# Sums of products by accumulating transfers, differences in place, and a projection with seven columns a head

## The chip, the cores and the metric

The kernel runs on one core of a Trainium2 chip. What is measured is the device time of one execution in microseconds. Differences of about 0.5% of this kernel's time can't be told from no change.

## The reference

Sixteen images x of 64 channels and 64x64 pixels, all in fp32. First three residual steps with two 3x3 convolutions, then a linear-attention block with eight heads of eight channels:

```python
for _ in range(3):
    t = jax.nn.relu(_conv(x, w1) + b1[None, :, None, None])
    x = x + (1.0 / 3.0) * (_conv(t, w2) + b2[None, :, None, None])
x = jax.nn.relu(x)

def _ln(t, w, b):                      # over the 8 channels of a head
    m = t.mean(-1, keepdims=True)
    s = jnp.std(t, axis=-1, ddof=1, keepdims=True)
    return w * ((t - m) / (s + EPS)) + b
qkv = jnp.einsum('oc,bchw->bhwo', qkv_w, x)        # -> q, k, v per head
k, v = _ln(k, kln_w, kln_b), _ln(v, vln_w, vln_b)
kv = jnp.einsum('bhnd,bhne->bhde', k, v) / N
o = jnp.einsum('bhnd,bhde->bhne', q, kv)           # heads back to channels
ret = o + x
u = gelu(jnp.einsum('oc,bchw->bohw', o1_w, ret))
return gelu(jnp.einsum('oc,bchw->bohw', o2_w, u) + x)
```

## The kernel before

**Tiles.** Two images make a pair: 128 partitions are two images of 64 channels. There are eight pairs, three x tiles in a ring (`xs`), one tile t between the two convolutions of a step, and one program of ten iterations. In each iteration a pair enters (step 0), the pair before it is in steps 0 and 1, and the one before that in step 2 and in its attention; so convolutions of one pair stand beside the attention of another.

**Phases and gaps.** An iteration has six phases with 42 gaps in all (`GAPS`); in each gap TensorE runs one unit of a convolution or half a unit. CONV0 (x to t) is a direct convolution of nine taps (line 956) in "long" units, or in its "short" half by products. CONV1 (t to x's increment dx) is by products throughout. A product half takes a column of input rows, spreads it on VectorE into six planes v (SPREAD, lines 711 to 771), multiplies the planes on TensorE (line 982 for CONV1, 989 for the short half of CONV0) in three parts of two planes, and merges the six results into four output rows on VectorE (MERGE, lines 786 to 829). ScalarE drains each part out of PSUM: parts 0 and 1 into `m`, part 2 into `m_ends` (lines 551 to 554). `m` is a single buffer: the next half's part 0 waits until the sums have been made from it. MERGE starts with two operations of 128x1024, sum and difference of the halves of m (lines 793, 794), into `sums`.

**Attention steps.** PIXELS (line 586, ScalarE) copies x, PROJECT k (line 1021, TensorE) makes k and v of an eighth of the pixels with the pixels as stationary operand and the 128 columns of `kvw` as moving one, ScalarE copies them to `kv` (598) and squares them (606), VectorE sums the squares of each head (836). The mean is taken out by the weights beforehand, so that only the deviation is left to be made: DEVIATION (610), INVERT (843 to 850), NORMALISE (855). OUTER (1033, TensorE) makes k'v, the four FOLD steps (1042 to 1050, with copies on VectorE at 859 to 871) turn it into a matrix, UP and DOWN (1064, 1073) apply it and the second weight with a gelu (618) between, VectorE adds x (881), FINISH (623) is the last gelu, RELU (591) the relu of x. In PSUM the convolutions have two buffers of two banks; the attention uses one slot in turn, and three in the last iteration.

**Order.** Each engine runs one hand-made order. The tables CONV_PLACES (for SPREAD, MERGE and RECTIFY of each half, by pair 0, pairs 1 to 6, pair 7) and LATE, LAST, FINAL (for the attention of pairs 0 to 5, of pair 6, of pair 7) give each step a gap as a number; within a gap the numbers order them. Every engine takes the steps in that order, and semaphores do the rest.

**GpSimd's queue.** GpSimd issues the additions of dx to x: two accumulating transfers a half (line 494), one for each side, in the order in which dx is made. The convolution of the next step waits for them (`x_added`). x comes in by SP's queue in four chunks of two transfers; w1 by two transfers on ScalarE's queue. The first unit of a pair waits for chunks 0 and 1.

## Time and profile before

| | us |
|---|---|
| median of the runs (1300.70, 1303.31, 1306.62) | 1303.31 |
| the profiled run | 1304.89 |
| its span | 1303.1 |
| TensorE busy in it | 1188.0 |
| VectorE busy | 1085.5 |
| ScalarE busy | 597.4 |
| GpSimd busy | 91.1 |
| granted clock, mean (1.00 is 2.4 GHz) | 0.967 |

The span is the time from the first to the last instruction in the trace; 1.8 us of the profiled run lie outside it. Busy times say how long an engine had an instruction under way. Matmuls overlap in TensorE, so a mean duration of one record is longer than what it adds to the time; what counts is the distance from one line's first start to the next line's. The stretches of 150 us from 350 to 1100 are alike, each a little more than one pair; the first 350 us hold the start and the last 200 the drain of the pipeline.

### The profile page before, as it was taken

What the parts mean: (1) busy time and instruction counts of PE and PEld (TensorE: products, weight loads), DVE (VectorE), ACT (ScalarE), POOL (GpSimd) and SP (SyncE); (2) the same over time, 40 slices, a digit from 0 to 9 for tenths busy, and PEclk for the clock granted to TensorE, in tenths of its full rate; (3) what the DMA queues carried; (4) which work ended last, traced back from release to release, by engine and by line L of the source; (5) the groups of instructions that cost most, each with busy time, mean ns of one, the idle gap of its engine ahead of it and who ended that gap; (6) DMA issues with size and microseconds to landing.
All of it is one profiled execution on the core that took longest, in us unless ns stands there. A gap on an engine that the chain in (4) does not pass through costs nothing. (4 is left out here: it accounts for less than half of the span.)

```text
span 1303.1 us, 40508 instructions
## 1 busy us (share of the span) xinstructions
PE 1188.0 (91%) x18613; PEld 805.4 (62%) x18613; DVE 1085.5 (83%) x1425; ACT 597.4 (46%) x642; POOL 91.1 (7%) x119
## 2 busy tenths in 40 slices
PE   6989999999999999999999999999999999785845
PEld 2546766577556766676566875676665875445432
DVE  3658888899888998899988997989978998987563
ACT  0212324454455626544455625554455625544573
POOL 2010110001010100101000100101000110110000
PEclk9989999999999999999999999999999999897876
DMA  7430330315061513515061422515061330430221
GB/s 131 91 68 1 69 68 2 68 36 102 18 150 33 102 36 99 101 36 102 2 164 35 86 52 70 129 35 102 2 163 36 69 69 34 100 68 2 82 51 65
DMA packets 87130, 88.95 MB, mean 68 GB/s; under 512 B 70320, under 2 KB 70320, under 8 KB 86960
## 3 DMA queue, kind: packets, MB, share of 16 engines
q0 software_dynamic: 13824, 51.91, 21.0%
q1 hardware_dynamic: 72496, 33.86, 10.3%
q8 instruction: 146, 2.39, 0.8%
q10 hardware_dynamic: 640, 0.59, 0.3%
q14 instruction: 24, 0.20, 0.0%
HBM read 17.66 MB, written 16.78 MB: 26 GB/s over the span
## 5 line engine op out<-in xcount | busy, mean ns | idle before, releaser
L956 PE MATMUL ps<-xs,w_t 64*64 64x512 f32 x4608 | 519.0, 594 | 10.2 <-DMA xs<-dx 6.3
L982 PE MATMUL ps<-v,fw 64*64 64x256 f32 x6912 | 398.9, 380 | 5.9 <-ACT m L552 4.1
L956 PEld LDWEIGHTS ps<-xs,w_t 64*64 64x64 f32 x4608 | 255.6, 134 | 224.1 <-issue 173.9
L982 PEld LDWEIGHTS ps<-v,fw 64*64 64x64 f32 x6912 | 302.2, 133 | 98.3 <-issue 18.4
L524 ACT ACTIVATE t<-ps,b_col 128x1024 f32<-128x1024 f32 x64 | 72.3, 1129 | 260.4 <-PE ps L956 204.9
L494 POOL DMA_DIRECT2D xs<-dx x96 | 83.4, 965 | 1154.3 <-DVE dx L829 1144.6
L722 DVE TENSOR_TENSOR q<-t 128x2112 f32<-128x2112 f32 x48 | 113.2, 2357 | 28.3 <-ACT t L524 15.4
L989 PE MATMUL ps<-v,sw 64*64 64x256 f32 x2304 | 134.4, 376 | 1.7 <-ACT t L524 1.7
L989 PEld LDWEIGHTS ps<-v,sw 64*64 64x64 f32 x2304 | 116.4, 132 | 21.5 <-issue 10.4
L554 ACT ACTIVATE m<-ps 128x1024 f32<-128x1024 f32 x80 | 82.2, 1028 | 65.6 <-PE ps L982 37.1
L836 DVE TENSOR_REDUCE rstd<-g 128x128 f32<-128x1024 f32 x64 | 77.1, 1216 | 38.7 <-ACT g L606 38.7
L554 ACT ACTIVATE m_ends<-ps 128x1024 f32<-128x1024 f32 x64 | 65.7, 1026 | 92.2 <-PE ps L982 59.7
L793 DVE TENSOR_TENSOR sums<-m 128x1024 f32<-128x1024 f32 x64 | 78.1, 1220 | 29.0 <-ACT m L554 29.0
L1021 PE MATMUL ps<-kvw,y 64*64 64x128 f32 x2048 | 75.5, 280 | 19.1 <-ACT y L586 15.7
L1021 PEld LDWEIGHTS ps<-kvw,y 64*64 64x64 f32 x2048 | 69.4, 139 | 34.7 <-ACT y L586 23.3
L598 ACT ACTIVATE kv<-ps 128x1024 f32<-128x1024 f32 x64 | 65.6, 1025 | 47.6 <-PE ps L1021 38.5
L881 DVE TENSOR_TENSOR y<-ps,xs 128x1024 f32<-128x1024 f32 x32 | 39.1, 1223 | 55.2 <-PE ps L1073 55.0
L768 DVE SCALAR_TENSOR_TENSOR v<-q 128x1056 f32<-128x1056 f32 x64 | 80.2, 1254 | 0.0
L794 DVE TENSOR_TENSOR sums<-m 128x1024 f32<-128x1024 f32 x64 | 78.1, 1221 | 0.0
L551 ACT ACTIVATE m<-ps,b_third 128x512 f32<-128x512 f32 x48 | 32.9, 685 | 76.5 <-DVE sums L794 39.8
L606 ACT ACTIVATE g<-ps 128x1024 f32<-128x1024 f32 x64 | 66.0, 1032 | 1.1 <-DVE rstd L836 1.1
L1033 PE MATMUL ps<-kv 64*64 64x64 f32 x2048 | 45.4, 231 | 21.6 <-DVE kv L855 21.6
(108 smaller groups left out, 1115.4 us busy)
## 6 DMA issues: line engine op xcount, KB each, us to landing
xs<-dx POOLq DMA_DIRECT2D x96, 528.0 KB, 6.1
xs<-in_x SPq DMA_DIRECT2D x64, 256.0 KB, 5.1
out<-y SPq DMA_DIRECT2D x32, 512.0 KB, 3.1
q<-in_L_conv_w ACTq DMA_DIRECT2D x2, 144.0 KB, 6.1
v<-in_L_conv_w ACTq DMA_DIRECT2D x2, 144.0 KB, 7.3
b_col<-in_L_conv_b ACTq DMA_DIRECT2D x4, 0.2 KB, 6.1
y<-in_L_conv_qkv_w SPq DMA_DIRECT2D x4, 16.0 KB
y<-in_L_conv_o_w SPq DMA_DIRECT2D x4, 16.0 KB
```

The source lines that it names most:

```text
L494: nc.gpsimd.dma_start(tile[:, row * PADDED:(row + 16) * PADDED], dx[h][:, side, :, :].rearrange("p r w -> p (r w)"), accum_op=ALU.add).the ...
L524: main = nc.scalar.activation(to, at, ACT.Relu, bias=b1_col[:, :])
L554: nc.scalar.activation(to, at, ACT.Copy, scale=factor).then_inc(drained, 1)
L722: vec.tensor_tensor(q[:, :, :], rows[:, at + 2:at + 18, :], rows[:, at:at + 16, :], ALU.subtract).then_inc(stepped, 1)
L768: vec.scalar_tensor_tensor(to[:, :, 4:6], step[:, :, 0:2], -4.0, step[:, :, 2:4], ALU.mult, ALU.add)
L793: vec.tensor_tensor(sums[:, 0:2, :], m[:, 0:4:2, :], m[:, 1:4:2, :], ALU.add)
L794: vec.tensor_tensor(sums[:, 2:4, :], m[:, 0:4:2, :], m[:, 1:4:2, :], ALU.subtract).then_inc(sums_made, 1)
L836: vec.tensor_reduce(rstd[k // 4][:, k % 4, :], squares[k % 2].rearrange("p i (h d) -> p (i h) d", d=HD), AX.X, ALU.add).then_inc(squares_s ...
L956: last = mm(to[CH * side:CH * side + CH, BANK * p:BANK * p + BANK], w1_t[half, tap, :], tile[half, rows, c:c + COLS], start=tap == 0, stop ...
L982: last = mm(to[CH * i:CH * i + CH, at:at + SPAN], fw[rows, product, c, :], from_t[rows, tiles, place, i, c:c + COLS], start=c == 0, stop=c ...
L989: last = mm(to[CH * side:CH * side + CH, at:at + SPAN], sw[rows, side, product, c, :], from_x[rows, tiles, place, c:c + COLS], start=c == ...
L1021: last = mm(ring_ps[SLOT[a, *s]][columns, at:at + P], pixels[k // 2 % 2][half, first:first + CH], kvw[half, :], start=True, stop=True)
```

## The change

1. `m` has two buffers and `sums` is gone. GpSimd adds the second part into the first in place by an accumulating transfer of 128x1024 (SUM, line 511), and VectorE makes the difference in place from it with one operation of the same size (line 835: -2 times part 1, plus the sum). ScalarE's drain of part 0 waits for the merge two halves before. The rest of MERGE is in a slightly different order: first what needs sums only.
2. GpSimd goes through one table order of SUM and ADD (the old pair of additions, line 520). SUM and ADD have numbers in CONV_PLACES.
3. `kvw` has 112 columns instead of 128: seven directions a head. These are the seven orthogonal to the mean in a rotated basis, so the sum of the seven squares is that of the eight deviations; the step that built the old centring builds the rotation (a few small operations at the start). PROJECT, the copy, the square and the reduction have seven eighths of their size.
4. The chunks of x end at rows 9, 16, 25 and 32 (before 8, 16, 24, 32); the first unit waits for chunk 0 alone; w1 comes by one transfer on SP's queue and one on ScalarE's.
5. All four tables have new numbers, so the steps stand in another order on every engine.

```diff
-        (SPREAD, CONV0, 1, 1): 24.81, (SPREAD, CONV0, 2, 1): 20.65, (SPREAD, CONV1, 0, 0): 8.16,
+        (SPREAD, CONV0, 1, 1): 27.7, (SPREAD, CONV0, 2, 1): 19.15, (SPREAD, CONV1, 0, 0): 5.42,
...
+        (SUM, CONV0, 1, 1): 26.54, (SUM, CONV0, 2, 1): 22.59, (SUM, CONV1, 0, 0): 11.11, (SUM, CONV1, 0, 1): 14.63,
...
-        m = sb("m", [P, 4, BANK])
+        m = [sb(f"m{k}", [P, 2, 2, BANK]) for k in range(2)]
...
-        kvw = sb("kvw", [P, P])
+        kvw = sb("kvw", [P, FREE])
...
+            sp.dma_start(w_raw[0][:, 0:CH * K * K], w1.rearrange("o c y x -> o (c y x)")).then_inc(w_in[0], 16)
...
+            def add_products(half):
+                plane = PLANE[half]
+                pool.wait_ge(drained, NUMBER[last_unit(half)])
+                nc.gpsimd.dma_start(m[plane % 2][:, 0].rearrange("p k e -> p (k e)"),
+                                    m[plane % 2][:, 1].rearrange("p k e -> p (k e)"), accum_op=ALU.add
+                                    ).then_inc(summed[plane % 2], 16)
...
+            for it, gap, _unit, _sub in GAPS:
+                for _a, s in todo(it, gap):
+                    if s[0] == SUM:
+                        add_products(s[1])
+                    elif s[0] == ADD:
+                        add_to_x(s[1])
...
-                    if part == 0 and plane:
-
-                        act.wait_ge(sums_made, plane)
-                    to = m[:, 2 * part:2 * part + 2, :].rearrange("p k (s e) -> p k s e", s=2)
+                    if part == 0 and plane >= 2:
+
+                        act.wait_ge(*merged(plane - 2))
+                    to = m[plane % 2][:, :, part, :].rearrange("p k (s e) -> p k s e", s=2)
...
-                dve.wait_ge(drained, NUMBER[unit])
-                vec.tensor_tensor(sums[:, 0:2, :], m[:, 0:4:2, :], m[:, 1:4:2, :], ALU.add)
-                vec.tensor_tensor(sums[:, 2:4, :], m[:, 0:4:2, :], m[:, 1:4:2, :], ALU.subtract
-                                  ).then_inc(sums_made, 1)
-                a_, c_, b_, d_ = (sums[:, k, :] for k in range(4))
+                total, b_and_d = m[plane % 2][:, 0], m[plane % 2][:, 1]
+                dve.wait_ge(summed[plane % 2], 16 * (plane // 2 + 1))
+                vec.scalar_tensor_tensor(b_and_d, b_and_d, -2.0, total, ALU.mult, ALU.add).then_inc(halved, 1)
...
-                        for c in ((0, 1), (2,), (3,), ())[b]:
+                        for c in ((0,), (1, 2), (), (3,))[b]:
...
-                                  last = mm(ring_ps[SLOT[a, *s]][columns, at:at + P],
+                                  last = mm(ring_ps[SLOT[a, *s]][columns, at:at + FREE],
```

On GpSimd the steady iterations held only the additions, two transfers a half. Before, in one such stretch (xs are x tiles, dx0 and dx1 the increments of the two halves):

```order
L494 DMA xs1<-dx0 128x1056 [waits dx_made]
L494 DMA xs1<-dx0 128x1056
L494 DMA xs1<-dx1 128x1056 [waits dx_made]
L494 DMA xs1<-dx1 128x1056
L494 DMA xs2<-dx0 128x1056 [waits dx_made]
L494 DMA xs2<-dx0 128x1056
```

Now (m0 and m1 are the two buffers of products):

```order
L511 DMA m1<-m1 128x1024 [waits drained]
L511 DMA m0<-m0 128x1024 [waits drained]
L511 DMA m1<-m1 128x1024 [waits drained]
L520 DMA xs2<-dx0 128x1056 [waits dx_made]
L520 DMA xs2<-dx0 128x1056
L511 DMA m0<-m0 128x1024 [waits drained]
L511 DMA m1<-m1 128x1024 [waits drained]
L520 DMA xs2<-dx1 128x1056 [waits dx_made]
L520 DMA xs2<-dx1 128x1056
```

The additions of the second half now stand behind two sums, and each of those waits for a drain of ScalarE.

On VectorE the fold of an attention stands behind the merge of a short half (outer_sb, half_affine: small matrices of the fold). Before:

```order
L859 COPY outer_sb<-ps 128x128 [waits outer_read]
L793 TENSOR_TENSOR sums<-m 128x1024 [waits drained,dx_made]
L794 TENSOR_TENSOR sums<-m 128x1024
L817 SCALAR_TENSOR_TENSOR t<-sums 128x4x64 [waits sums_made]
L817 SCALAR_TENSOR_TENSOR t<-sums 128x4x64
L819 TENSOR_TENSOR t<-sums 128x2x4x64
L823 SCALAR_TENSOR_TENSOR eo<-sums 128x512 [waits v_made]
L824 SCALAR_TENSOR_TENSOR eo<-sums 128x512
L828 TENSOR_TENSOR t<-eo,m_ends1 128x2x4x64 [waits drained,ends_made]
L829 TENSOR_TENSOR t<-eo,m_ends1 128x2x4x64
L864 COPY half_affine<-ps 64x64 [waits small_ready]
```

Now:

```order
L900 COPY outer_sb<-ps 128x128 [waits outer_read]
L835 SCALAR_TENSOR_TENSOR m1<-m1 128x1024 [waits summed1,dx_made]
L859 SCALAR_TENSOR_TENSOR eo<-m1 128x512 [waits v_made]
L861 SCALAR_TENSOR_TENSOR t<-m1 128x4x64 x2
L864 SCALAR_TENSOR_TENSOR eo<-m1 128x512 [waits halved]
L865 TENSOR_TENSOR t<-m1 128x2x4x64
L869 TENSOR_TENSOR t<-eo,m_ends1 128x2x4x64 [waits drained,ends_made]
L870 TENSOR_TENSOR t<-eo,m_ends1 128x2x4x64
L905 COPY half_affine<-ps 64x64 [waits small_ready]
```

The merge keeps its place before the fold's copy, is one large operation shorter, and waits for the transfer (summed1) where it waited for ScalarE.

On TensorE near the end, the last pair's third-step conv0 (line 956 before, 997 now), the projections (1021, 1062) and the first OUTER of pair 6 (1033, 1074). Before:

```order
L1021 MATMUL ps<-kvw,y1 64x128 [waits proj_taken,pixels_made]
L1021 MATMUL ps<-kvw,y1 64x128 x15
L1021 MATMUL ps<-kvw,y0 64x128 [waits proj_taken,pixels_made]
L1021 MATMUL ps<-kvw,y0 64x128 x15
L956 MATMUL ps<-xs1,w1_t 64x512 [waits drained,x_added0]
L956 MATMUL ps<-xs1,w1_t 64x512 x19
L1033 MATMUL ps<-kv 64x64 [waits small_taken,normalised]
L1033 MATMUL ps<-kv 64x64 x15
```

Now:

```order
L1062 MATMUL ps<-kvw,y1 64x112 [waits proj_taken,pixels_made]
L1062 MATMUL ps<-kvw,y1 64x112 x15
L1074 MATMUL ps<-kv 64x64 [waits small_taken,normalised]
L1074 MATMUL ps<-kv 64x64 x15
L1062 MATMUL ps<-kvw,y0 64x112 [waits proj_taken,pixels_made]
L1062 MATMUL ps<-kvw,y0 64x112 x15
L997 MATMUL ps<-xs1,w1_t 64x512 [waits drained,x_added0]
L997 MATMUL ps<-xs1,w1_t 64x512 x19
```

OUTER and one projection now stand ahead of the conv0 that stood ahead of OUTER.

## Rows read from the trace of the kernel before

**Rows 1.** The page, first section: each engine's busy time, share, instructions

```profile
PE 1188.0 (91%) x18613; PEld 805.4 (62%) x18613; DVE 1085.5 (83%) x1425; ACT 597.4 (46%) x642; POOL 91.1 (7%) x119
```

**Rows 2.** Stretches: window, length, busy of five engines, clock, DMA share, GB/s

```profile
650.00:800.00 150.00, 146.18 (x2356) 101.26 (x2351) 133.96 (x172) 75.41 (x82) 10.41 (x12) 1.00 0.35 73
1100.00:1303.00 203.00, 135.52 (x2404) 90.28 (x2396) 142.56 (x184) 103.95 (x109) 10.43 (x12) 0.81 0.25 62
```

**Rows 3.** TensorE's waits in 650 to 800: total, times, longest

```profile
PE ps L1073 <- ACT g L618: 2.7, 2, 1.4
...
PE ps L1048 <- DVE kv_head L866: 0.6, 1, 0.6
```

**Rows 4.** Groups by line, count | busy, mean ns of one | idle before

```profile
L793 DVE TENSOR_TENSOR sums<-m 128x1024 f32<-128x1024 f32 x64 | 78.1, 1220 | 29.0 <-ACT m L554 29.0
L836 DVE TENSOR_REDUCE rstd<-g 128x128 f32<-128x1024 f32 x64 | 77.1, 1216 | 38.7 <-ACT g L606 38.7
L1021 PE MATMUL ps<-kvw,y 64*64 64x128 f32 x2048 | 75.5, 280 | 19.1 <-ACT y L586 15.7 <-ACT g L606 3.4
L1021 PEld LDWEIGHTS ps<-kvw,y 64*64 64x64 f32 x2048 | 69.4, 139 | 34.7 <-ACT y L586 23.3 <-issue 9.6
L598 ACT ACTIVATE kv<-ps 128x1024 f32<-128x1024 f32 x64 | 65.6, 1025 | 47.6 <-PE ps L1021 38.5 <-PE ps L1033 9.1
L552 ACT ACTIVATE m<-ps 128x512 f32<-128x512 f32 x48 | 28.3, 590 | 0.0
```

**Rows 5.** Timeline of TensorE in the steady regime: start, duration, line, [idle before]

```profile
647.68 1.09 PE L1073 MATMUL ps<-g,o 64*64 64x512 f32 x8 [1.42 <-ACT g L618]
...
683.06 1.11 PE L1021 MATMUL ps<-kvw,y 64*64 64x128 f32 x32
683.93 4.56 PE L956 MATMUL ps<-xs,w_t 64*64 64x512 f32 x40
...
796.20 1.09 PE L1073 MATMUL ps<-g,o 64*64 64x512 f32 x8 [1.43 <-ACT g L618]
```

**Rows 6.** Line 494, the additions: issue on GpSimd, and landing

```profile
L494 POOL DMA_DIRECT2D xs<-dx x96: 843/867/1222, 65.6 to 1245.4; - x96
...
DMA to landing us min/median/max: 4.5/6.1/9.6
```

**Rows 7.** Timeline round a fold: drain, merge, fold

```profile
768.33 1.03 ACT L554 ACTIVATE m<-ps 128x1024 f32<-128x1024 f32 x1 [1.58 <-PE ps L989]
...
773.81 1.22 DVE L793 TENSOR_TENSOR sums<-m 128x1024 f32<-128x1024 f32 x1
...
779.42 0.69 DVE L829 TENSOR_TENSOR t<-eo,m_ends 128x512 f32<-128x512 f32 x1
...
781.42 0.33 PE L1048 MATMUL ps<-q_w,kv_head 64*64 64x64 f32 x4 [0.55 <-DVE kv_head L866]
```

**Rows 8.** Timeline of TensorE at the head

```profile
13.77 10.76 PE L956 MATMUL ps<-xs,w_t 64*64 64x512 f32 x72 [3.91 <-DMA xs<-in_x]
...
73.55 6.88 PE L956 MATMUL ps<-xs,w_t 64*64 64x512 f32 x44 [6.32 <-DMA xs<-dx]
```

**Rows 9.** Timeline of TensorE in the tail

```profile
1102.15 2.82 PE L982 MATMUL ps<-v,fw 64*64 64x256 f32 x48
...
1154.85 4.54 PE L956 MATMUL ps<-xs,w_t 64*64 64x512 f32 x40
1160.85 0.69 PE L1033 MATMUL ps<-kv 64*64 64x64 f32 x32 [1.45 <-DVE kv L855]
...
1193.63 3.60 PE L1033 MATMUL ps<-kv 64*64 64x64 f32 x128 [9.00 <-DVE kv L855]
```

**Rows 10.** Timeline of ScalarE in the last stretch

```profile
1239.26 1.04 ACT L586 ACTIVATE y<-xs 128x1024 f32<-128x1024 f32 x1
...
1262.03 1.94 ACT L591 ACTIVATE xs<-xs 128x2048 f32<-128x2048 f32 x1
```

**Rows 11.** The chain that ended last: start, duration, what

```profile
1240.35 2.03 PE ps L1021 x32
```

## What the change will do to the time

> **What bounds the kernel now.** I read the engines' busy time first: TensorE 1188.0 of 1303.1 us, VectorE 1085.5, ScalarE 597.4, GpSimd 91.1 [rows 1]. An average over stages says little, so the stretches come next. In the one from 650 to 800 us, which stands for four like it between 350 and 1100, TensorE is busy 146.18 of 150 us at a granted clock of 1.00 (2.4 GHz) and VectorE 133.96; in the last 203 us TensorE is busy 135.52 only, at a mean clock of 0.81, between the two levels [rows 2]. So there are two regimes. In the steady one TensorE is the bound, and the list of its waits holds 3.9 us a period: two of 1.4 for a gelu, and two of 0.6 inside the fold (one of them is shown) [rows 3]. A period (one pair of images) is 148.5 us: the same down-projection starts at 647.68 and at 796.20 [rows 5]. In the last 200 us nothing is left to fill TensorE's gaps, and a chain through all engines decides. A microsecond off VectorE is therefore worth nothing in the first regime unless it stands in front of one of those waits; a column off TensorE is worth its time; and in the second regime everything on the chain counts.
>
> **Projection in seven directions.** Thirty-two records of it with 128 columns take from 683.06 to 683.93, when the next line's matmuls start: 0.87 us [rows 5]. With 112 columns an eighth goes: 0.11 us, eight times a pair, 0.87 us. Six pairs are projected in the steady regime: -5.2 us. The bounds are 0 (the weight loads, whose number stays, set the pace) and -6.9 (all eight pairs by that amount). I take 5.2, because these loads are under matmuls in this stretch: TensorE runs on into the next line without a gap [rows 5]. On ScalarE the copy and the square lose 128 of 1024 elements. A copy of 512 takes 590 ns and one of 1024 takes 1025 [rows 4], so 0.85 ns an element and 0.11 us each; VectorE's reduction loses an eighth of 1216 ns [rows 4], 0.15 us. In the steady regime both lie under TensorE and bring nothing.
>
> **Sums by transfers.** VectorE loses two operations of 1.22 us in a merge (the second has the same form as the first) and gains one of the same size and type [rows 4]: about -1.15 us with the overlap of neighbours, eight merges a pair, -9.2, and with the reductions' 8 x 0.15 -10.4, so VectorE falls from 134 to about 123 us in 150. That is off the path. What it costs is latency: the merge no longer starts when ScalarE has drained part 1, but when a transfer of 512 KB has landed. The trace holds no such transfer alone. Its nearest rows are the accumulating transfers of 528 KB, issued in pairs: 4.5 us at least, 6.1 in the middle, 9.6 at most, 0.84 us or more on GpSimd to issue [rows 6]. I take 4.6 to 5, near the shortest, since a lone transfer shares the rings with no twin.
>
> Where does that reach TensorE? I walked every merge. Most have their v planes a whole phase ahead. The tight place is the last half of the third step's conv0: its merge stands right ahead of the fold, and the fold's small matmuls wait for VectorE's copies behind it. Before, part 1 is drained at 769.36, the merge runs from 773.81 to 780.1, the fold's copy follows at once, and TensorE waits 0.55 us at 781.42 [rows 7]. After, the merge is 1.15 us shorter, so it may start at 774.96 and end no later: that is 5.6 us after the drain. A sum that lands in 4.6 to 5 us fits; one of 6.1 costs 0.5. The double-buffered m moves ScalarE's drain from waiting for the last merge's sums to waiting for the merge before that one, which has ended by then. On GpSimd's queue an addition to x may now stand behind a sum that still waits for its drain. Who waits for that addition is the conv0 of the next step and the spread for its short half, and in the steady regime another pair's phase lies between; I price it at nothing there and at the sum's own 4.6 us at the head, where no other pair is. Sum for the steady waits: 0, with bounds of -15 (two thirds of 3.9 x 6 us gone) and +24 (below).
>
> **Loads at the head.** TensorE starts its first convolution at 13.77 after waiting 3.91 us for x [rows 8]. The first unit now needs one chunk instead of two, and w1 comes by two queues: I take 3.0 of the 3.91. At 73.55 TensorE waits 6.32 us for the first addition to x [rows 8], and on that chain stands a sum (+4.6) and two merges one operation shorter (-2.3). So -3.0 + 4.6 - 2.3 = -0.7 (bounds -3 and +3).
>
> **Order at the end.** I measure from 1102.15, the conv1 products that both orders have there. Before, the last pair's third-step conv0 starts at 1154.85, and four microseconds later OUTER of pair 6 waits until 1160.85 [rows 9]. After, that OUTER and a projection stand ahead of the conv0, and VectorE's spread for the last pair stands behind a DOWN's addition and a merge more. So conv0 cannot start before about 1163: +8. TensorE idles 9.00 us at 1193.63 for the next NORMALISE [rows 9]; it takes up some 4.5 of the 8 by my walk, and the last products come 3.5 later, PIXELS of the last pair 3.3 later. Bounds: +8 (nothing absorbed) and -5 (the attention of pair 6, earlier now, empties that wait).
>
> **Last stretch.** From the end of the first PIXELS at 1240.30 to the end 62.8 us remain [rows 10]. RELU 0, 1.94 us of ScalarE between two projections' drains at 1262.03 [rows 10], moves behind them: -1.8 (the next drain starts a little before its end). Sixteen drains at 0.11: -1.75. Projections at the lower clock take 2.03 us [rows 11]; an eighth of four that stand on the chain: -1.0. Four reductions at 0.15: -0.6. Together -5.2 (bounds -2 and -7).
>
> **Sum.** -0.7 - 5.2 + 0 + 3.3 - 5.2 = -7.8 us. The span goes from 1303.1 to 1295.3, the profiled run from 1304.89 to 1297.1; the median shown is 1.6 below the profiled run, so 1295.5.
>
> **Rivals.** (1) *The waits go.* Seven per cent less work on VectorE and a merge that is shorter lets the fold and the gelus come early, and two thirds of the 3.9 us a period vanish: -15, 1280.5. For it: VectorE at 134 of 150 is not far from being the bound. Against it: two of the waits are for ScalarE's gelu [rows 3], which the change does not shorten.
> (2) *The columns save nothing.* If the weight loads pace the projection, the 5.2 and the 1.0 don't come: 1301.7, no difference. For it: a load takes 139 ns on average and the mean matmul record 280 [rows 4], no wide margin where several matmuls run at once. Against it: no gap at 683.93 [rows 5].
> (3) *Late sums, slower.* The sum lands as late as the slowest accumulating transfer, 9.6 us [rows 6], because it queues behind an addition's pair or its descriptors are written late. At the fold that is 9.6 - 5.6 = 4.0 us in each of six periods: +24, 1319.5. It decides from a landing of 5.6 us on. For it: the middle of the row, 6.1, is above that already. Against it: those transfers go in twos, and a sum at the fold has no twin.
> The Trainium skill speaks for (3): its page "SBUF — State Buffer", section "SBUF: two separate sides", says that GpSimd cannot write a transfer's descriptors while VectorE runs an operation in a two-port mode, so the transfer seems blocked by VectorE. No row here shows a transfer issued by GpSimd against an idle VectorE, so the trace leaves it open. Against (3) stands its page "DMA: Bandwidth & Descriptors", section "Anatomy of one DMA — SWDGE (gpsimd) path": about 2.0 us and the bytes at 436 GB/s, by which 512 KB would be an estimated 3.2 us, and the sum above about 1294; no row of the trace is below 4.5.
>
> **How the numbers follow.** Forecast 1295.5 with its own range of 1288 to 1302: 0.45, two thirds of it below 1296.8. Rival 1: 0.20. Rival 2: 0.17. Rival 3: 0.18. A measurement tells about 0.5% (6.5 us) from no change, so faster means below 1296.8: 0.30 + 0.20 = 0.50; the same 0.15 + 0.17 = 0.32; slower, above 1309.8, 0.18. The range of 1279 to 1312 leaves out three quarters of rival 3 and a quarter of rival 1.
>
> **What would show it.** Projections of 32 records in 0.76 us; VectorE near 123 of 150 us in the steady stretches, TensorE still near 146 in them; sums that land in 4.6 to 5 us and TensorE's waits in 650 to 800 still under 5 us. A list of waits that names the transfer of the sums, or a fold wait of several microseconds, proves rival 3; a list that is empty proves rival 1. In the tail: the last pair's third-step conv0 61 us behind the conv1 products from which I measure (before 52.7), RELU 0 behind the drains. I am wrong on the whole if the periods are longer or shorter than 147.6 us by more than 1 us.

## The result, and the profile after

The changed kernel takes 1321.11 us (median; 1319.32 to 1322.55) against 1303.66: the ratio is 1.0133, with an interval from 1.0107 to 1.0160. It is slower by 17.4 us, where 7.8 us less were forecast, and it lies above the range of 1279 to 1312. The profiled run has 1319.32 us and a span of 1317.1.

The first lines of its page, engines' busy time and GpSimd's queue (packets, MB, share of the 16 DMA engines), answer to [rows 1]:

```profile
PE 1190.7 (90%) x18613; PEld 875.9 (66%) x18613; DVE 996.7 (76%) x1365; ACT 584.6 (44%) x642; POOL 146.7 (11%) x183
...
q0 software_dynamic: 23040, 85.47, 34.2%
```

VectorE lost 88.8 us of work and ScalarE 12.8, as worked out ahead; GpSimd's queue went from 51.91 to 85.47 MB. And the time went up. The stretch of 650 to 800 us (columns as in [rows 2]) says it again:

```profile
650.00:800.00 150.00, 144.79 (x2322) 111.00 (x2316) 123.46 (x164) 72.79 (x80) 17.37 (x20) 0.99 0.49 101
```

VectorE has 123.46 for 133.96, and TensorE did fewer of its records (2322 for 2356) in the same 150 us, at a mean clock of 0.99 for 1.00.

**Where the time went.** A steady kernel is best laid against another at a mark that both pass: here the first conv0 matmul of an iteration (line 956 before, 997 after), found by counting that line's records. In us from the span's start:

| | first matmul | third iteration | eighth iteration | end |
|---|---|---|---|---|
| before | 13.8 | 229.8 | 972.4 | 1303.1 |
| after | 8.3 | 232.3 | 980.2 | 1317.1 |
| after against before, in this part | -5.5 | +8.0 | +5.3 | +6.2 |

So the 14.0 us between the two spans have three sources. The head gained 5.5 us and then lost 8.0. Before, each of the five steady iterations lasts 148.52 us; after, they last 149.84, 150.20, 149.80, 149.96 and 148.16, where 147.65 was forecast. And the drain of the pipeline is 6.2 us longer.

**The head.** Who waits for the sums (line 511), and how long they take to land, by that line's view:

```profile
L511 POOL DMA_DIRECT2D m<-m x64: 841/857/1552, 51.3 to 1245.0; - x64
...
  DVE m L835: 78.9, 23
...
DMA to landing us min/median/max: 4.5/5.2/11.4
```

A sum lands in 5.2 us in the middle, just above the 4.6 to 5 that I took. But VectorE waits 78.9 us for sums, 23 times. All eight sums ahead of the third iteration are waited for, 44.5 us of the 78.9, and in the second iteration they follow on each other. Four of them on the timeline of VectorE:

```profile
148.89 1.23 DVE L835 SCALAR_TENSOR_TENSOR m<-m 128x1024 f32<-128x1024 f32 x1 [4.73 <-DMA m<-m]
...
156.24 1.23 DVE L835 SCALAR_TENSOR_TENSOR m<-m 128x1024 f32<-128x1024 f32 x1 [2.44 <-DMA m<-m]
...
165.58 1.23 DVE L835 SCALAR_TENSOR_TENSOR m<-m 128x1024 f32<-128x1024 f32 x1 [4.43 <-DMA m<-m]
...
189.65 1.23 DVE L835 SCALAR_TENSOR_TENSOR m<-m 128x1024 f32<-128x1024 f32 x1 [3.96 <-DMA m<-m]
```

Four merges, 15.6 us of waiting: there is only one pair ahead of this one, nothing else to do, and every step waits for the one before it. The wait that the forecast did price, TensorE's for the first addition to x, came out near it: 9.27 us for 6.32 [rows 8], +2.95 where 4.6 - 2.3 = 2.3 was taken.

```profile
70.33 17.58 PE L997 MATMUL ps<-xs,w_t 64*64 64x512 f32 x144 [9.27 <-DMA xs<-dx]
```

**The periods.** TensorE's waits from 350 to 1100 us, total, times and longest. First the waits for the gelu in the kernel before ([rows 3] has those of a fifth of that stretch), then the list after; line 1073 is 1114 there:

```profile
PE ps L1073 <- ACT g L618: 15.0, 11, 1.4
```

```profile
PE ps L1114 <- ACT g L652: 6.4, 5, 1.3
PE ps L1074 <- issue: 4.4, 3, 2.3
PE ps L1086 <- DVE half_affine L905: 4.4, 5, 0.9
PE ps L1062 <- issue: 2.9, 3, 1.5
PE ps L1091 <- DVE mix L910: 2.8, 5, 0.6
PE ps L1089 <- DVE kv_head L907: 2.8, 5, 0.6
```

Three things are new. The fold waits three times a period, not twice: 2.0 us in all for 1.1. "issue", a wait for nothing that the profile shows, is there with 8.4 us (1.1 of it on a line not shown), and was absent before. And after the fold the granted clock falls in three of the five periods. Against that, the waits for the gelu fell from 15.0 to 6.4 us. Over the five periods from mark to mark TensorE's waits come to 24.3 us for 19.9, and the lower clock takes 5.1 for nothing before. What is left, TensorE's own work, is 4.2 less, about the projection's part. Together that is the +5.3. These are TensorE at one fold and the window just behind it:

```profile
489.14 0.33 PE L1086 MATMUL ps<-v_affine,half_affine 64*64 64x64 f32 x4 [0.85 <-DVE half_affine L905]
490.03 0.33 PE L1089 MATMUL ps<-q_w,kv_head 64*64 64x64 f32 x4 [0.56 <-DVE kv_head L907]
490.93 0.37 PE L1091 MATMUL ps<-o_t,mix 64*64 64x64 f32 x2 [0.56 <-DVE mix L910]
```

```profile
490.00:495.00 5.00, 4.41 (x32) 2.03 (x36) 3.95 (x6) 1.60 (x1) 0.00 (x0) 0.66 0.01 3
```

A clock of 0.66 over 5 us is 3.4 us at the lower of the two levels (1.2 GHz), so 1.7 us of work lost. Before, at the same place, the fold waited twice 0.55 and the clock stayed at 1.00 in all five periods.

**The end.** TensorE, at the conv1 products from which I measured, at the spread that was moved, at pair 6's first OUTER, and at the first PROJECT of the last pair (its counterpart is in [rows 11]):

```profile
1114.64 2.81 PE L1023 MATMUL ps<-v,fw 64*64 64x256 f32 x48
...
1142.24 9.78 PE L1023 MATMUL ps<-v,fw 64*64 64x256 f32 x144 [7.52 <-DVE v L812]
...
1175.26 1.13 PE L1074 MATMUL ps<-kv 64*64 64x64 f32 x32 [11.63 <-DVE kv L896]
...
1261.15 3.27 PE L1062 MATMUL ps<-kvw,y 64*64 64x112 f32 x64 [3.37 <-ACT y L618]
```

From the mark to that PROJECT it is 146.5 us for 138.2 before: +8.3. From there to the end it is 55.95 for 62.75: -6.8. The remaining +4.7 lies in the eighth iteration up to the mark.

### The profile page after: what moved, and what is told of

The parts are those of the page before. It is cut to its first block and busy times, and to the rows that moved or that the text cites. A ratio compares the mean times of both kernels' runs of the same rounds, so it can differ in the third digit from the quotient of the medians.

```text
span 1317.1 us, 40504 instructions
## 1 busy us (share of the span) xinstructions
PE 1190.7 (90%) x18613; PEld 875.9 (66%) x18613; DVE 996.7 (76%) x1365; ACT 584.6 (44%) x642; POOL 146.7 (11%) x183
## 3 DMA queue, kind: packets, MB, share of 16 engines
q0 software_dynamic: 23040, 85.47, 34.2%
## 5 line engine op out<-in xcount | busy, mean ns | idle before, releaser
L997 PE MATMUL ps<-xs,w_t 64*64 64x512 f32 x4608 | 530.0, 600 | 12.3 <-DMA xs<-dx 9.3
L997 PEld LDWEIGHTS ps<-xs,w_t 64*64 64x64 f32 x4608 | 291.6, 135 | 199.3 <-issue 138.7
L1023 PEld LDWEIGHTS ps<-v,fw 64*64 64x64 f32 x6912 | 337.6, 133 | 75.0 <-issue 24.3
L511 POOL DMA_DIRECT2D m<-m x64 | 59.1, 924 | 892.1 <-ACT m L586 892.1
L835 DVE SCALAR_TENSOR_TENSOR m<-m 128x1024 f32<-128x1024 f32 x64 | 78.1, 1220 | 78.9 <-DMA m<-m 78.9
L877 DVE TENSOR_REDUCE rstd<-g 128x128 f32<-128x896 f32 x64 | 68.8, 1082 | 79.3 <-ACT g L640 79.3
L631 ACT ACTIVATE kv<-ps 128x896 f32<-128x896 f32 x64 | 58.9, 920 | 84.0 <-PE ps L1062 74.9
L1062 PEld LDWEIGHTS ps<-kvw,y 64*64 64x64 f32 x2048 | 72.7, 142 | 25.4 <-ACT y L618 13.8
L1062 PE MATMUL ps<-kvw,y 64*64 64x112 f32 x2048 | 75.0, 270 | 14.0 <-ACT y L618 11.1
L1074 PEld LDWEIGHTS ps<-kv 64*64 64x64 f32 x2048 | 47.0, 145 | 30.3 <-DVE kv L896 24.2
L618 ACT ACTIVATE y<-xs 128x1024 f32<-128x1024 f32 x32 | 33.6, 1053 | 68.2 <-DMA xs<-dx 68.2
```

What stands on the lines that cost most here:

```text
L835: vec.scalar_tensor_tensor(b_and_d, b_and_d, -2.0, total, ALU.mult, ALU.add).then_inc(halved, 1)
L877: vec.tensor_reduce(rstd[k // 4][:, k % 4, :].rearrange("p (i g) -> p i g", i=2), squares[k % 2][:, :, 0:4 * FREE].rearrange("p i (g d) -> ...
L997: last = mm(to[CH * side:CH * side + CH, BANK * p:BANK * p + BANK], w1_t[half, tap, :], tile[half, rows, c:c + COLS], start=tap == 0, stop ...
L1023: last = mm(to[CH * i:CH * i + CH, at:at + SPAN], fw[rows, product, c, :], from_t[rows, tiles, place, i, c:c + COLS], start=c == 0, stop=c ...
L1062: last = mm(ring_ps[SLOT[a, *s]][columns, at:at + FREE], pixels[k // 2 % 2][half, first:first + CH], kvw[half, :], start=True, stop=True)
L1074: last = mm(outer_ps[image_half[i], part, :], kv[rows, k % 4, i, j, 0, :], kv[rows, k % 4, i, j, 1, :], start=k == 0 and j == 0, stop=k == ...
```

## The experiments

All ratios are against runs of the kernel before on the same chip. "Head", "period" and "drain" are the parts of the table above: up to the start of the third iteration, one of the five steady iterations behind it, and from the start of the eighth to the end.

**The projection alone**, put into the kernel before.

```diff
-        kvw = sb("kvw", [P, P])
+        kvw = sb("kvw", [P, FREE])
...
-                                  last = mm(ring_ps[SLOT[a, *s]][columns, at:at + P],
+                                  last = mm(ring_ps[SLOT[a, *s]][columns, at:at + FREE],
```

> The kernel before with the projection in seven directions alone. Theory (the columns pace the projection): a period of 148.52 us becomes 147.65, six of them -5.2, and the last stretch loses some 3 us to shorter drains; about 1295. Rival (weight loads pace it): periods stay 148.5, about 1301.

1293.27 us, ratio 0.9926 (0.9913 to 0.9938). Periods of 147.52 for 148.52: a full microsecond, a little more than the columns' 0.87. The columns pace the projection, and rival 2 is out. In the changed kernel too, 32 records take 0.77 us, from the one row's start to the next:

```profile
1151.85 0.93 PE L1062 MATMUL ps<-kvw,y 64*64 64x112 f32 x32
1152.62 2.77 PE L1023 MATMUL ps<-v,fw 64*64 64x256 f32 x48
```

**Projection and loads**, in the kernel before.

```diff
-                        for c in ((0, 1), (2,), (3,), ())[b]:
+                        for c in ((0,), (1, 2), (), (3,))[b]:
...
+            sp.dma_start(w_raw[0][:, 0:CH * K * K], w1.rearrange("o c y x -> o (c y x)")).then_inc(w_in[0], 16)
```

> The kernel before with the projection in seven directions and the new loads (chunks, first unit on chunk 0 alone, w1 by two queues). Theory (the chain of the first two iterations starts at the first unit): the 4 to 5 us by which the first convolution starts earlier stay, 1289. Rival (given back at the first wait for an addition to x): 1293, as with the projection alone.

1290.11 us, ratio 0.9894 (0.9875 to 0.9913). The third iteration starts at 223.5 for 227.3 with the projection alone; periods of 147.52 to 147.56. The start stays won, and two of the change's five parts are worth 13.8 us together.

**A transfer that nobody waits for**, in the kernel before.

```diff
+            def move_idle(half):
...
+                pool.wait_ge(drained, NUMBER[last_unit(half)])
+                if PLANE[half]:
+                    pool.wait_ge(idle_moved, 16 * PLANE[half])
+                nc.gpsimd.dma_start(idle[:, :], fw.rearrange("p k c o -> p (k c o)")[:, 0:2 * BANK], accum_op=ALU.add
+                                    ).then_inc(idle_moved, 16)
```

> The kernel before, and GpSimd issues one more accumulating transfer of 512 KB for each half when its part 1 is drained, into a tile that nobody reads or waits for; all else as before. Theory (the transfers' traffic itself holds up TensorE's instruction stream): waits of TensorE for nothing that the profile shows appear between 350 and 1100 us, 4 to 10 us in all, periods go from 148.52 to 149.5 or more, about 1311. Rival (only the wait for the sums costs): no such waits, periods 148.5, 1303.

1310.15 us, ratio 1.0048 (1.0035 to 1.0062). 6.3 us, but not as the theory had it: waits for nothing visible make 1.0 us in 350 to 1100 (0.77 and 0.19), and three of the five periods stay within 0.2 of 148.52 (148.52, 149.80, 149.08, 148.56, 148.72). 4.0 us are lost between the first matmul and the third iteration. Not in the waits for additions to x: the first is 6.59 us for 6.32. There TensorE waits 4.69 us for ScalarE's t where it waited 1.74, and the lower clock takes 8.5 us for 5.1; why is not shown. So the traffic has a price, but in the old order it hardly stops TensorE in the periods.

**Sums back on VectorE**, in the changed kernel.

```diff
-                dve.wait_ge(summed[plane % 2], 16 * (plane // 2 + 1))
+                dve.wait_ge(drained, NUMBER[unit])
+                vec.tensor_tensor(total, total, b_and_d, ALU.add).then_inc(summed[plane % 2], 1)
+                dve.wait_ge(summed[plane % 2], plane // 2 + 1)
```

> The changed kernel with the sums back on VectorE (one more operation of 128x1024 in each merge, no transfer for them), in the same order. Theory: the third iteration, which starts at 232.3, starts some 8 us earlier, since three sums in a row stand on the chain there; TensorE's waits for nothing visible (8.4 us from 350 to 1100) go; the fold's merge is 1.15 us longer, so that the fold waits longer and the clock falls there in every period, +1.5 each; about 1312. Rival (the transfers cost nothing, the order does all): the start unchanged and 1.15 us more at each fold, about 1327.

1332.43 us, ratio 1.0225 (1.0211 to 1.0239): slower than the change by 11. The head is 12.5 us shorter (third iteration at 219.8), more than expected; but the periods are 152.3 to 154.0. The wait list of 380 to 1100:

```profile
PE ps L1086 <- DVE half_affine L905: 15.3, 5, 3.2
```

One more operation of 1.22 us in each merge makes the wait at the fold 3.1 us for 0.9 and lowers the clock in every period. The drain is 8.2 us longer too. So in the new order VectorE, with 10 us less to do a pair, has no slack ahead of the fold: the timeline of the changed kernel has it running without a pause from INVERT through four NORMALISE steps, a spread and the merge to the fold's copy. The old order has the same steps there, without a pause too and with that one operation more, and its fold waits 1.1 us. The new order is built on the lighter VectorE and gives nothing for it.

**The first FOLD one unit earlier**, in the changed kernel.

```diff
-    ... (FOLD, 0): 29.02, ...
+    ... (FOLD, 0): 28.98, ...
```

> The changed kernel with the first FOLD one unit earlier for pairs 0 to 5 (28.98 for 29.02), so that a unit of conv0 stands between it and the second FOLD, as before the change. Theory: the wait of 0.86 us ahead of the second FOLD goes, and with 1.1 us of waits for 2.0 the clock stays at its upper level there: 1.5 us on average in each of six periods, about 1312. Rival (VectorE's copy is late in any case): the wait moves to the next FOLD and the clock falls as before, 1320.

1319.19 us, ratio 1.0126 (1.0104 to 1.0147): no change, the rival's. TensorE now does a unit between the two FOLD steps and waits all the same, and the clock falls as before:

```profile
636.83 3.61 PE L997 MATMUL ps<-xs,w_t 64*64 64x512 f32 x29
641.32 0.33 PE L1086 MATMUL ps<-v_affine,half_affine 64*64 64x64 f32 x4 [0.88 <-DVE half_affine L905]
```

**PROJECT 7 earlier**, in the changed kernel, so that VectorE's run ahead of the fold starts earlier.

```diff
-    ... (PROJECT, 7): 22.1, ...
+    ... (PROJECT, 7): 20.95, ...
```

> The changed kernel with PROJECT 7 of pairs 0 to 5 one to two gaps earlier (20.95 for 22.1). Theory (VectorE runs without a pause from that projection's squares to the fold's copies): its chain starts 4 us earlier, the wait ahead of the second FOLD goes, 1.1 us of waits for 2.0, the clock stays up; 1 to 1.7 us in each of six periods, about 1312. Rival (the additions to x, or the sum of the half ahead of the fold, hold VectorE instead): periods stay at 149.8, 1320.

1319.79 us, ratio 1.0134 (1.0117 to 1.0151): no change in the time, but not in the mechanism. The timeline of VectorE at a fold:

```profile
636.67 1.22 DVE L835 SCALAR_TENSOR_TENSOR m<-m 128x1024 f32<-128x1024 f32 x1 [1.96 <-DMA m<-m]
...
642.42 0.46 DVE L905 COPY half_affine<-ps 64x64 f32<-64x64 f32 x2 [0.85 <-PE ps L1083]
```

VectorE is early now. It first waits 1.96 us for the sum, as rival 3 had it, and then 0.85 for TensorE: the wait ahead of the second FOLD is down to 0.55. So VectorE's late start is what lengthened the wait at that FOLD. The time stays the same even so: the clock falls in three of the five periods as before, and the waits for nothing visible are 8.9 us from 380 to 1100. Whether both edits at once would bring the fold back was not run.

**The sums left out**, in the changed kernel: no transfers, and the merge goes on at the drain.

```diff
-                dve.wait_ge(summed[plane % 2], 16 * (plane // 2 + 1))
+                dve.wait_ge(drained, NUMBER[unit])
...
-                    if s[0] == SUM:
-                        add_products(s[1])
-                    elif s[0] == ADD:
+                    if s[0] == ADD:
```

> The changed kernel without the sums: the 64 transfers are not issued, and each merge goes on when part 1 is drained, with products that are not added (that part of the computation is left out). Order and VectorE's work as in the changed kernel. Theory (latency at the head, traffic in the periods): the third iteration starts at 219 to 220 instead of 232.3; TensorE's waits for nothing visible between 350 and 1100 fall from 8.4 to below 4 us; about 1300. Rival (the transfers cost only at the head, the rest is the order): periods stay at 149.6, about 1308.

1302.72 us, ratio 1.0004 (0.9990 to 1.0017). Eighteen microseconds less than the change: in this order the sums cost more than the whole loss. The third iteration starts at 218.1 for 232.3, so 14.2 of them lie in the head. The waits for nothing visible inside the projections, the OUTER steps and the products behind them are gone: one of 0.5 us is left. But the periods, 147.5 to 150.7, are not shorter on average, since another wait appeared, at the second unit of an iteration:

```profile
375.64 8.01 PE L995 MATMUL ps<-xs,w_t 64*64 64x512 f32 x72 [2.10 <-issue]
```

That unit needs the second and third chunk of x. The transfers of SP's queue (two stores of y and four loads of x), first before the change, then in this kernel:

```profile
367.69 3.02 SPq L444 DMA_DIRECT2D out<-y  x2
370.76 4.46 SPq L421 DMA_DIRECT2D xs<-in_x  x4
```

```profile
356.68 7.07 SPq L464 DMA_DIRECT2D out<-y  x2
363.79 8.01 SPq L440 DMA_DIRECT2D xs<-in_x  x4
```

Before, the loads went out 7.5 us ahead of the iteration's start (378.3); here 1.8 ahead (365.6). FINISH 3 had been moved from 37.68 to 39.6, its store waits for it, and the loads of the pair that enters next stand behind the store. The changed kernel's loads go out just as late (380.34, with the iteration's start at 382.11), and there no such wait shows.

**FINISH 3 earlier**, in the kernel without sums and in the changed one.

```diff
-    (DOWN, 2): 37.15, (DOWN, 3): 38.02, (FINISH, 3): 39.6,
+    (DOWN, 2): 37.15, (DOWN, 3): 38.02, (FINISH, 3): 38.1,
```

> The kernel without the sums (that part of the computation is left out), with FINISH 3 at 38.1 for 39.6. Theory: the waits of 2 to 3 us at the second unit of each iteration are for loads of x behind a late store; they go, and periods of 150.3 become 148 to 148.4: about 1292. Rival (these waits have another cause): 1302.

> The changed kernel with FINISH 3 of pairs 0 to 5 at 38.1 for 39.6, so that its store, and the loads of x that stand behind the store on SP's queue, go out some 5 us earlier. Theory: with the sums' transfers there is no wait for those loads in the periods, so nothing changes, 1319 to 1321. Rival (late loads are part of what the periods lose): 1 us a period, 1313.

Without sums 1296.15 us, ratio 0.9950 (0.9928 to 0.9972): 6.6 us less, and the waits at the second unit are gone. The theory had 1292 for it and the rival 1302; it lies between. With sums 1324.9, ratio 1.0175 (1.0146 to 1.0204): no gain, and 4 to 6 us above the expectation, though the interval overlaps the change's. The periods of the first average 149.2, of the second 150.3: with the same order, the sums cost 1.0 us a period. Between these two runs they cost 29 us in all, where it was 18 between the change and the kernel without sums, so what they cost depends on where FINISH 3 stands.

The first, with no sums at all and no late loads, is 1.7 above the 147.52 of projection and loads in the old order: 0.9 a period for the third wait of the fold, 0.7 for the clock (it falls in two of the five periods), about 1.0 for new waits for ScalarE's drains, less 1.4 for the waits for the gelu, and some 0.5 of small waits and rest. But the waits for drains in the conv1 products came with FINISH 3 at 38.1: neither the changed kernel nor the one without sums lists them. And the first period without sums, ahead of the first late load, is 147.45, no longer than in the old order. So the order's own price is not settled; it lies between nothing and 1.7 us a period.

**The same traffic, not waited for**, in the changed kernel: the 64 transfers of the second diff above at the sums' places, into the tile that nobody reads; the sums are left out.

> As the kernel without the sums, but with the 64 transfers issued at their old places into a tile that nobody waits for: traffic without the wait. Theory (the traffic holds up TensorE's instruction stream): head within 2 us of the kernel without sums, waits for nothing visible back at about 8 us, periods 1 to 1.5 us longer than there, 6 to 9 us in all. Rival (the traffic costs nothing, only the wait for the landing does): the same time as without sums, within 2 us.

1351.17 us, ratio 1.0368 (1.0344 to 1.0393): far above both expectations, and so no clean test. Each of these transfers waits for the last one, and GpSimd stood 19.2 us in six such waits, with additions to x behind them; 24.6 us went in five waits at the second unit of an iteration, where x had not landed (its loads took up to 14.6 us). One thing it does show: the waits inside the projections, the OUTER steps and the products behind them, gone without sums, are back (seven, 9.6 us).

**The first eight sums on VectorE**, the other 56 by transfers.

```diff
+EARLY = [half for half in PRODUCTS if any(it < 2 and unit == last_unit(half) for it, _g, unit, _s in GAPS)]
...
+                if half in EARLY:
+                    dve.wait_ge(drained, NUMBER[unit])
+                    vec.tensor_tensor(total, total, b_and_d, ALU.add).then_inc(early_summed, 1)
+                    dve.wait_ge(early_summed, EARLY.index(half) + 1)
...
```

> The changed kernel with the sums of the first eight halves (those that end in the first two iterations) on VectorE, by one more operation of 128x1024 each; the other 56 by transfers. Theory (the sums' landing stands in a row there): the third iteration starts at 219 to 221 for 232.3, the rest as in the changed kernel, about 1309. Rival (what the head loses comes back in later waits): 1318 or more.

1310.25 us, ratio 1.0060 (1.0037 to 1.0083): 10.9 us less than the change, the third iteration at 220.4. Up to there the head is settled: its loss is the landing of eight sums. What it is worth at the end is less sure: the profiled run was the slowest of the six (1314.55), and in it the five periods last 151.55 us on average, with the clock lower in all five, so part of the gain was lost again behind the head, as the rival had it.

**The old order with the sums**: all parts of the change but its tables.

```diff
+        found.append((GAP_OF[(*last_unit(half)[:3], last_unit(half)[3] - 1)] + 1.5, a, (SUM, half)))
...
+            found.append((min(max(base + conv_places[MERGE, conv, s, h] + 1.3, GAP_OF[(*last_unit(half)[:3], last_unit(half)[3] - 1)] + 2.6), 10 * GAP_COUNT - 1), a, (ADD, half)))
```

> The changed kernel (sums by transfers, projection, loads) with the tables of before; a sum stands on GpSimd's queue behind the gap of its unit, an addition behind its merge. To be set against the kernel before with projection and loads alone. Theory (VectorE was not the bound in the old order): the sums cost 10 to 12 us in the first two iterations and a few us in waits for nothing visible, and bring nothing in the periods: 1300 to 1304. Rival (only the new order is slow, the sums help): at or below 1289.

1530.17 us, ratio 1.1743 (1.1723 to 1.1764). Neither theory came near. By the view of the sums' line:

```profile
  DVE m L826: 362.7, 57
...
DMA to landing us min/median/max: 4.5/7.3/11.0
```

VectorE waits for 57 of 64 sums, 6.4 us each. In the old order a merge stands right behind its drain, and VectorE takes its steps in order, so it waits out every landing, with everything else behind it. How much of the 6.4 is my queue order on GpSimd (a sum behind an addition that waits for a merge) is open. What it shows is that the new order is no free choice: the sums need a step's distance between drain and merge.

**The spread of the last pair earlier**, alone, and with its merge and rectify.

```diff
-        ... (SPREAD, CONV1, 1, 0): -2.57 ...
+        ... (SPREAD, CONV1, 1, 0): -4.33 ...
```

```diff
-        ... (MERGE, CONV0, 1, 1): 37.36 ...
-        ... (RECTIFY, CONV0, 1, 1): 38.83 ...
-        ... (SPREAD, CONV1, 1, 0): -2.57 ...
+        ... (MERGE, CONV0, 1, 1): 36.7 ...
+        ... (RECTIFY, CONV0, 1, 1): 37.05 ...
+        ... (SPREAD, CONV1, 1, 0): -4.33 ...
```

> The changed kernel with one spread of the last pair (second step's conv1, first half) back at its old place, two gaps earlier. Theory: VectorE does it in the 10 us in which it idles for two down-projections at 1110 to 1122, TensorE's wait of 7.5 us at 1142 goes, and the last pair comes 6 to 8 us earlier, 1313. Rival (the attention of pair 6 on VectorE sets the end in any case): the wait moves to the next OUTER, 1320.

> The changed kernel with three steps of the last pair earlier: the merge of its second step's conv0 ahead of a down-projection's addition (36.7 for 37.36), its rectify on ScalarE at 37.05 for 38.83, the spread behind it at its old place. Theory (in the run before, the spread was earlier but its merge still stood behind that addition): VectorE no longer idles 5.7 us ahead of the merge, and the last pair comes 6 to 8 us earlier, about 1312. Rival (the attention of pair 6 sets the end): about 1320.

1324.47 (1.0169, 1.0151 to 1.0188) and 1326.32 (1.0173, 1.0153 to 1.0194): no gain; their medians are 3 to 5 us above the change's, with intervals that overlap. The wait of 7.5 us for the spread went, and this came on ScalarE and TensorE, in the second of the two:

```profile
1149.15 1.06 ACT L618 ACTIVATE y<-xs 128x1024 f32<-128x1024 f32 x1 [11.04 <-DMA xs<-dx]
```

```profile
1151.33 4.59 PE L1023 MATMUL ps<-v,fw 64*64 64x256 f32 x48 [6.86 <-ACT m L584]
```

The spread now stands ahead of pair 6's merge; its addition to x comes later; PIXELS of pair 6 waits for that on ScalarE, and the drains of the last pair's products stand behind PIXELS. Both pairs need VectorE there, and OUTER still waits 11.63. What a better order of the drain would be stays open. In the kernel before, the last pair's third-step merge starts 78.4 us behind the mark and its next spread 93.2; in the changed one 96.5 and 106.0. The two edits moved an earlier spread, and none moved these two back.

**Projection, loads and the last pair's table**, in the kernel before.

```diff
 FINAL = {
-    (PIXELS, 0): 42.27, (PROJECT, 0): 43.97, (PIXELS, 1): 46.96, (PROJECT, 1): 47.48, (PROJECT, 2): 47.86,
+    (PIXELS, 0): 44.21, (PROJECT, 0): 45.35, (PIXELS, 1): 45.72, (PROJECT, 1): 49.61, (PROJECT, 2): 50.13,
...
-    (OUTER, 0): 62.56, (NORMALISE, 3): 62.74, (RELU, 0): 62.77, (PROJECT, 6): 62.93, (OUTER, 1): 63.81,
+    (RELU, 0): 69.14, (NORMALISE, 7): 69.15, (OUTER, 7): 71.04, (RELU, 1): 72.43, (FOLD, 0): 73.09, (FOLD, 1): 73.43,
```

> The kernel before with the projection, the new loads and the changed kernel's table for the last pair's attention (RELU 0 behind the drains, and another order of its last steps). Theory: the last stretch, 6.8 us shorter in the changed kernel, of which some 3 us are the projection's, loses 3 to 4 us more: 1286. Rival (the last stretch became shorter only because the pair came later): 1290.

1286.61 us, ratio 0.9877 (0.9863 to 0.9891). This is the version that beats both: 16 us under the kernel before and 34 under the change, with the sums on VectorE and the old order in the periods. The table is worth 3.5 us by the medians and 2.2 by the ratios, and the intervals of the two versions overlap, so its worth is not shown.

## Why the prediction was wrong

**Term by term**, in us of the span. The mark between the second row and the third is the conv1 products from which the prediction measured (1102.15 before, 1114.64 after).

| part | forecast | measured |
|---|---|---|
| head, to the third iteration | -0.7 | +2.5 |
| projection and steady waits, from there to the mark | -5.2 + 0 | +10.0 |
| order at the end, from the mark to the last pair's first PROJECT | +3.3 | +8.3 |
| last stretch | -5.2 | -6.8 |
| sum | -7.8 | +14.0 |

The largest step that failed is the term "sum for the steady waits: 0". With the projection's -5.2 it stands for +15: TensorE's waits in that stretch came to 30.5 us for 23.6, and the lower clock takes 8.5. The sign that the prediction set for itself came true: the periods are 149.6 on average, and four of the five are off 147.6 by more than 1 us.

**By the ratios.** Against the kernel before, the runs give: projection -9.6 us, loads -4.2 more, the new order with one VectorE operation less a merge +14.3 (of which 7 are late loads of x), the sums' transfers +17. These add up to the +17.4, since each is the difference of two neighbouring runs. Each price holds for the order in which it was taken: with FINISH 3 moved, the sums cost 29.

**Right: the projection.** Term -5.2 for six periods; it measured 1.00 a period. The mechanism and the size hold. The rest of the 9.6 lies in the head (2.5 us by the third iteration's start) and the drain, and was not taken apart.

**Right: the last stretch. Wrong: what the end absorbs of the new order.** For the stretch -5.2 was forecast and -6.8 measured. In the order, conv0 of the last pair stands 63.0 us behind the mark, for 61 forecast and 52.7 before: the +8 came as +10.3. What failed is the absorption, 4.5 of the 8 us in the wait of 9.00 that TensorE had at 1193.63 [rows 9]. These are TensorE and VectorE there, before and after:

```profile
1195.30 2.35 DVE L722 TENSOR_TENSOR q<-t 128x2112 f32<-128x2112 f32 x1
...
1204.11 0.69 PE L982 MATMUL ps<-v,fw 64*64 64x256 f32 x2
```

```profile
1177.66 5.63 PE L997 MATMUL ps<-xs,w_t 64*64 64x512 f32 x40
...
1208.96 2.50 PE L1074 MATMUL ps<-kv 64*64 64x64 f32 x128 [2.49 <-DVE kv L896]
...
1220.64 2.36 DVE L763 TENSOR_TENSOR q<-t 128x2112 f32<-128x2112 f32 x1
...
1227.87 4.42 PE L1023 MATMUL ps<-v,fw 64*64 64x256 f32 x48 [2.09 <-DVE v L812]
```

The wait did shrink, to 2.49, and the fold of pair 6 comes only 1.1 us later behind the mark. (The 11.63 further up is another wait, ahead of pair 6's first OUTER.) But the last pair got none of it. Its spread now stands behind NORMALISE and fold copies of pair 6, 106.0 us behind the mark for 93.2, and its conv1 products start 113.2 behind it for 102.0. So its PIXELS come 8.3 later, my upper bound. This is read from the two traces; no run moved that spread back.

**Right in kind, too small: the head.** -0.7 was made of -3.0, one sum of 4.6 and two shorter merges of -2.3. The -3.0 was 5.5, and the chain with one sum in it, that of the first iteration up to the first addition to x, cost 2.95 for 2.3. But only that chain was priced. The second iteration has no more pairs to fill in than one, and its six halves follow on each other. Two runs price all of it: 14.2 us with the sums left out, 11.9 with eight of them on VectorE. The step that failed here is the term "one sum on the chain"; eight was the count.

**Wrong: the steady regime at 0.** I took the fold from the trace of before, gave it the shorter merge, and found that a sum may land 5.6 us after the drain. That was true as far as it went: in the changed kernel VectorE does not wait for that sum at all. But VectorE comes to that merge later than before. Its steps at one fold, from INVERT (L843, now L884) to the fold's copy, before and after:

```profile
463.70 0.63 DVE L843 TENSOR_SCALAR kv<-rstd 128x512 f32<-128x512 f32 x1
...
482.98 0.45 DVE L864 COPY half_affine<-ps 64x64 f32<-64x64 f32 x2
```

```profile
468.94 1.09 DVE L877 TENSOR_REDUCE rstd<-g 128x128 f32<-128x896 f32 x1 [3.60 <-ACT g L640]
470.72 0.65 DVE L884 TENSOR_SCALAR kv<-rstd 128x512 f32<-128x512 f32 x1 [0.70 <-ACT rstd L644]
...
488.64 0.45 DVE L905 COPY half_affine<-ps 64x64 f32<-64x64 f32 x2
```

The run of steps is the same, and 1.4 us shorter, as forecast (17.9 for 19.3). But it starts 3.2 us later in its iteration (88.6 for 85.4 behind the first conv0 matmul), since the tables moved PROJECT 7 from 19.29 to 22.1 and VectorE waits 3.60 us for the last square. The copy comes 106.5 us behind that matmul for 104.7, and nothing in my sum priced that. The run with PROJECT 7 earlier confirms it: there VectorE is early, and the wait ahead of the second FOLD is down to 0.55. The two other parts of the +15, the waits for nothing visible (10.0 us up to the mark) and the clock, were not in the sum at all. The waits for the gelu gave 7.3 back. The five periods came out 5.3 us above those before, and 10.3 in all above five of 147.52; that lies inside the -15 to +24 that I gave the waits, but the price came by another way.

**Rival 3 had the sign, and not the place.** It had the sum late at the fold in each period. The sums are late, 14 us worth, at the head. At the fold one only is when VectorE has been made earlier, in the run with PROJECT 7 moved. The Trainium skill's rule that spoke for it ("SBUF — State Buffer", "SBUF: two separate sides") has GpSimd held up in writing descriptors while VectorE runs an operation in a two-port mode. In the changed kernel three sums that were issued and landed with VectorE idle took 4.5 to 4.6 us (at 94.50, 215.53 and 1237.23), and six with VectorE busy throughout, and nothing else of GpSimd's under way, 4.6 to 5.2: a difference of 0.7 us at most. Whether VectorE's operations there were in the mode that the page means, no run shows. The Trainium skill's rule that spoke against it ("DMA: Bandwidth & Descriptors", "Anatomy of one DMA — SWDGE (gpsimd) path") would make an estimated 3.2 us of 512 KB; the trace has 4.5 at least and 5.2 in the middle for the 64 sums, and 7.3 in the middle in the old order.

**Rival 1 was partly right.** Its -15 did not come, but of the two waits for a gelu in a period one went, against the reason given that the change does not shorten them.

**Not looked at: SP's queue.** The prediction had no term for a store that moves; the diff had FINISH 3 go from 37.68 to 39.6. Without the sums the late loads cost 6.6 us. In the changed kernel the loads go out as late and no wait for them shows; why is open. A cost that hides behind another is found only when the first is taken away.

## What to carry to other kernels

A transfer that replaces an instruction trades busy time for latency. Price it at each place where the consumer has nothing else to do, above all in the first and last iterations, by counting how many stand in a row there; a steady state that hides it says nothing about them. And work taken from an engine that is not the bound is worth only what the new order makes of it: set the new order's own price (here between nothing and 1.7 us a period) against it, by running the order without the new work and the new work's parts without the order. Such prices need not add up: the sums cost 18 us in one order and 29 in another that differs by one step's place.

## What the runs showed of the hardware

**TensorE's instruction stream waits behind transfers.** TensorE stood still in the middle of one step's matmuls, with no semaphore to wait for:

```profile
600.65 0.63 PE L1074 MATMUL ps<-kv 64*64 64x64 f32 x27 [1.74 <-issue]
```

These are the DMA queues in the 3.7 us up to that moment (packets, MB, share of the 16 engines); q8 carries instructions:

```profile
q0 software_dynamic: 172, 0.60, 85.5%
q8 instruction: 1, 0.02, 1.6%
```

There are nine such waits in the changed kernel between 300 and 1050 us, of 0.4 to 2.3 us, 10.0 in all. GpSimd's queue held the DMA engines for 78 to 99% of the 3.7 us ahead of each end, and in all nine one instruction transfer of 16,384 bytes ended 1.3 to 1.6 us before the wait did. What they have in common is their place in the stream. The trace has 146 of these transfers for some 37,470 instructions of TensorE (matmuls, weight loads and semaphores), so about 256 instructions each. Counted by that, all nine waits stand at a number that leaves 192 or 193 when it is divided by 256. So do the 72 other such waits of all the kernels here between 250 and 1250 us, apart from those at the second unit of an iteration, where x was late. So these waits stand at ends of blocks of the instruction stream.

How long they are goes with the traffic. With the sums left out all but one (0.52 us) are gone, with idle transfers in their place they are back; in the old order idle transfers make two up to 1050 us, of 0.77 and 0.19, and sums four, of 0.3 to 1.8. A full queue is not needed: the new order with its sums on VectorE has three, of 0.2 to 0.9, and ahead of these and of the four GpSimd's queue held 19 to 66% of the engines. Why most block ends cost nothing, no run here shows. The Trainium skill, page "Runtime: NRT & Kernel Launch", section "Instruction fetch mechanics", says that the fetch, in blocks of 16 KiB (256 instructions) over a DMA queue of the engine's own, is mostly hidden. The trace agrees with the block's size, and at these nine places the fetch is not hidden, with up to 2.3 us a time.

**The same short waits went with a lower clock in some kernels and not in others.** At the fold of the changed kernel 0.86, 0.56 and 0.56 us of idle time within 4 us were followed by the lower level of 1.2 GHz for 3.4 us in three of five periods. In the kernel with FINISH 3 earlier and the sums, the same three waits (0.86, 0.56, 0.56) were followed by no fall in any period. Two of 0.55 never were in the five kernels with the old order and the sums on VectorE. So the three waits alone do not decide it, and what else does is not shown. The waits cost 0.9 us more, the clock 1.7 more when it falls.
